# Softmax of a graph attention layer on 80 partitions instead of 8, merged with the edge sums, match matrices built one stage earlier

## The reference

```python
h = (x @ W.T).reshape(n, h_, d_)
e = leaky_relu(e_src + e_dst, 0.2) * (1.0 + et_emb[edge_type]) * edge_weight[:, None]
e_max = zeros((n, h_)).at[dst].max(e)          # largest logit of each destination and head, at least 0
e = exp(e - e_max[dst])
e_sum = zeros((n, h_)).at[dst].add(e)
alpha = e / (e_sum[dst] + 1e-10)
msg = h_src * alpha[:, :, None]
out = zeros((n, h_, d_)).at[dst].add(msg)      # then + x, a layer norm, gamma, beta
```

## Time and profile before

| | us |
|---|---|
| median of three runs (lowest, highest) | 2835.7 (2834.29, 2839.29) |
| the profiled execution's own time | 2833.69 |
| its span in the trace | 2832.0 |
| message stage, first instruction to the barrier's end | 1617.2 to 1842.5 |
| softmax stage | 1842.5 to 1891.7 |
| sums stage | 1891.7 to 1967.9 |

### The profile page before, as it was taken

One profiled execution on the slowest core, in us unless ns is written; L12 is line 12 of the kernel. 1 busy time (PEld: TensorE's weight loads), 2 busy tenths in 40 slices (PEclk: granted clock), 3 DMA queues, 4 the chain that ended last, 5 costly groups with the idle time before them and its releaser, 6 DMA issues. The chain is left out here.

```text
span 2832.0 us, 39727 instructions
## 1 busy us (share of the span) xinstructions
PE 2395.1 (85%) x13447; PEld 2050.2 (72%) x13447; DVE 1575.8 (56%) x3039; ACT 1093.6 (39%) x1874; POOL 856.0 (30%) x734
## 2 busy tenths in 40 slices
PE   5979999999999599999999799935777267999466
PEld 5969898989989599999999688824332155777355
DVE  4643233232323466666666533377799666777554
ACT  2233333333434233343333356623565353333232
POOL 1001010101000211111111134328898345665566
PEclk9989999999999799999999889968888688999788
DMA  6101010101002422333333234305466385776444
GB/s 218 37 8 56 19 56 19 51 19 44 26 23 49 159 104 104 112 110 104 118 138 119 86 102 118 89 25 198 140 224 226 130 260 187 260 263 233 154 152 130
DMA packets 118708, 330.52 MB, mean 117 GB/s; under 512 B 25981, under 2 KB 39293, under 8 KB 100571
## 3 DMA queue, kind: packets, MB, share of 16 engines
q1 hardware_dynamic: 69128, 228.79, 22.3%
q0 software_dynamic: 42976, 99.29, 12.2%
q10 hardware_dynamic: 6530, 1.53, 0.3%
HBM read 247.97 MB, written 128.49 MB: 133 GB/s over the span
## 5 line engine op out<-in xcount | busy, mean ns | idle before, releaser
L136 PE MATMUL b_y_ps<-W23h,b_Rh 128*128 128x320 f32 x800 | 249.5, 312 | 0.0
L138 PE MATMUL b_y_ps<-W23h,b_Rl 128*128 128x320 f32 x800 | 246.1, 308 | 0.0
L137 PE MATMUL b_y_ps<-W23l,b_Rh 128*128 128x320 f32 x800 | 246.0, 308 | 0.0
L537 POOL DMA_INDIRECT b_X<-in_x,b_idx x40 | 40.1, 1002 | 630.4 <-PE b_tp_ps L717 619.8
L911 POOL DMA_INDIRECT c_G<-T,c_idx x80 | 83.8, 1047 | 455.2 <-DVE c_U L1012 432.9
L136 PE MATMUL b_hid_ps<-b_hTh,W1h 128*128 128x512 f32 x500 | 200.6, 401 | 7.9 <-ACT b_Rh L586 7.9
L136 PE MATMUL c_u_ps<-c_W3h,c_hTh 128*128 128x320 f32 x640 | 200.8, 314 | 0.0
L137 PE MATMUL b_hid_ps<-b_hTl,W1h 128*128 128x512 f32 x500 | 199.3, 399 | 0.0
L138 PE MATMUL b_hid_ps<-b_hTh,W1l 128*128 128x512 f32 x500 | 199.2, 398 | 0.0
L138 PE MATMUL c_u_ps<-c_W3h,c_hTl 128*128 128x320 f32 x640 | 197.7, 309 | 0.0
L137 PE MATMUL c_u_ps<-c_W3l,c_hTh 128*128 128x320 f32 x640 | 197.7, 309 | 0.0
(11 more groups left out here) (378 smaller groups left out, 6971.7 us busy)
## 6 DMA issues: line engine op xcount, KB each, us to landing
c_X<-in_x SPq DMA_DIRECT2D x21, 1024.0 KB, 5.2
x<-n_O SPq DMA_DIRECT2D x20, 1032.0 KB, 4.9
g_X<-x SPq DMA_DIRECT2D x20, 1032.0 KB
x<-c_XB SPq DMA_DIRECT2D x20, 1028.0 KB, 3.9
n_X<-x SPq DMA_DIRECT2D x20, 1028.0 KB, 7.4
x<-g_O SPq DMA_DIRECT2D x20, 1024.0 KB, 3.9
c_XB<-in_x SPq DMA_DIRECT2D x19, 1024.0 KB
out<-g_B SPq DMA_DIRECT2D x19, 1024.0 KB, 4.8
```

Source lines behind the costliest of these rows:

```text
L136: pe.matmul(out, ah, bh, start=first, stop=False)
L137: pe.matmul(out, ah, bl, start=False, stop=False)
L138: return pe.matmul(out, al, bh, start=False, stop=last)
L537: pool.indirect_dma_start(X[:, i // GROUP, i % GROUP, :], None, a["x"][:, :], bass.IndirectOffsetOnAxis(idx[:, i:i + 1], 0), bounds_check= ...
```

## The change

1. Softmax and sums become one stage, `layer1_sums`, without the barrier between them. `logit` now has the shape 128 x (4 tiles of a group, 8 heads, 10 groups), so that the 80 columns of one j are turned at once: four transposes give `L` as 80 partitions (head by group, a "chunk") with 512 edge places each.
2. `same`, the two scans, the subtraction and Exp run on 80 x 512. A scan starts anew in each chunk, so the maxima have to be carried over: two scans of `same` alone (`left`, `right`) say whether a place is linked to the chunk's edge; four small matmuls bring the four edge values of each chunk to one partition (`rows`, 1 x 320); two scans over 80 values there chain the chunks (`before`, `after`); two matmuls bring the results back to 80 partitions (`cols`); and two passes apply `top = max(link * col, top)`.
3. ScalarE runs Exp once on a single column at the stage's start (`warm`), ahead of the copy of the logits.
4. The probabilities are split into `Ph` and `Pl` once for all tiles. GpSimd's copy of 8 columns goes; `Y`, `Yh` and `Yl` are 512 wide; the matmuls with `match` and `heads` become 256 wide, and each tile gets four more matmuls with 8 columns. The product reads its 8 factors at a distance of 10 elements.
5. The ten instructions that build `match` move to the start of the message stage.

```diff
@@ layer1_messages, vector @@
-                    dve.tensor_tensor(logit[:, bass.ds(g * 4, GROUP), :], dots[:, :, :], keep["fac"][:, bass.ds(g * 4, GROUP), :],
-                                      ALU.mult).then_inc(dot_read, 1)
-
+                    dve.tensor_tensor(logit[:, :, :, bass.ds(g, 1)], dots[:, :, :].unsqueeze(3),
+                                      keep["fac"][:, bass.ds(g * 4, GROUP), :].unsqueeze(3), ALU.mult).then_inc(dot_read, 1)
+
+                for g in range(EG):
+                    w = slice(g * GROUP, (g + 1) * GROUP)
+                    dve.tensor_tensor(match[:, w, :], keep["rows"][:, g * (GROUP * P):(g + 1) * (GROUP * P)].rearrange("p (j q) -> p j q", q=P),
+                                      over(keep["dst"][:, w].unsqueeze(2), [P, GROUP, P]), ALU.is_equal).then_inc(built, 1)
                 split_on_dve(dve, Wraw[:, :, :], Wh[:, :, 0:F], Wl[:, :, 0:F], w_hi, 1, w_lo)
...
@@ layer1_sums (layer1_softmax is gone); CH = EG * HEADS = 80, CW = GROUP * P = 512 @@
+        L, top = sb("L", [CH, CW]), sb("top", [CH, CW])
+        same = sb("same", [CH, CW + 1], U16)
+        left, right = sb("left", [CH, CW]), sb("right", [CH, CW])
...
             def _(act):
+                act.activation(warm[:, :], keep["eps"][:, 0:1], ACT.Exp)
+                act.wait_ge(turned, 1)
+                act.copy(L[:, :], turn[0:CH, :]).then_inc(flat, 1)
+                act.wait_ge(shifted, 1)
+                act.activation(L[:, :], L[:, :], ACT.Exp).then_inc(exped, 1)
+                act.wait_ge(prob_ready, 2)
+                act.copy(Ph[:, :, :, :], logit[:, :, :, :]).then_inc(p_hi, 1)
...
             def _(pool):
-                pool.wait_ge(init, 1)
+                pool.wait_ge(prob_ready, 2)
...
-                                           over(prob[:, bass.ds(t, 1), :].rearrange("p o h -> p (o h)").unsqueeze(2), [P, HEADS, HD]),
+                                           over(logit[:, j, :, bass.ds(g, 1)], [P, HEADS, HD]),
                                            ALU.mult).then_inc(weighed, 1)
-                        pool.tensor_copy(Y[:, j, :, F:F + HEADS], prob[:, bass.ds(t, 1), :]).then_inc(weighed, 1)
...
             def _(dve):
...
+                dve.tensor_tensor_scan(left[:, :], on, on, 1.0, ALU.mult, ALU.mult).then_inc(linked, 1)
+                dve.tensor_tensor_scan(right[:, ::-1], on_back, on_back, 1.0, ALU.mult, ALU.mult).then_inc(linked, 1)
+                dve.wait_ge(flat, 1)
+                dve.tensor_tensor_scan(top[:, :], on, L[:, :], 0.0, ALU.mult, ALU.max).then_inc(local, 1)
+                dve.wait_ge(local, 1)
+                dve.tensor_tensor_scan(top[:, ::-1], on_back, top[:, ::-1], 0.0, ALU.mult, ALU.max).then_inc(local, 1)
+
+                dve.wait_ge(rows_ready, 1)
+                dve.tensor_copy(rows[:, :], turn[0:1, 0:4 * CH]).then_inc(rows_out, 1)
+                dve.wait_ge(rows_out, 1)
+                tails, through, firsts, through_back = (rows[:, k * CH:(k + 1) * CH] for k in range(4))
+                dve.tensor_tensor_scan(before[:, 1:CH + 1], through, tails, 0.0, ALU.mult, ALU.max).then_inc(chained, 1)
...
+                dve.wait_ge(cols_ready, 1)
+                dve.tensor_copy(cols[:, :], back[0:CH, 320:324]).then_inc(cols_out, 1)
...
+                dve.scalar_tensor_tensor(out=top[:, :], in0=left[:, :], scalar=cols[:, 0:1], in1=top[:, :],
+                                         op0=ALU.mult, op1=ALU.max).then_inc(topped, 1)
...
+                dve.tensor_tensor(L[:, :], L[:, :], top[:, :], ALU.subtract).then_inc(shifted, 1)
+                dve.wait_ge(back_ready, 1)
+                dve.tensor_copy(flat_prob, back[:, 0:GROUP * CH]).then_inc(prob_ready, 1)
+                dve.wait_ge(prob_ready, 1)
+                dve.memset(flat_prob[0:1, :], 0.0).then_inc(prob_ready, 1)
+                dve.wait_ge(p_hi, 1)
+                dve.tensor_tensor(Pl[:, :, :, :], logit[:, :, :, :], Ph[:, :, :, :].bitcast(F32), ALU.subtract).then_inc(p_lo, 1)
...
             def _(pe):
+                for j in range(GROUP):
+                    mm = pe.transpose(turn[0:CH, j * P:(j + 1) * P], flat_prob[:, j * CH:(j + 1) * CH], keep["ident"][:, :])
+                mm.then_inc(turned, 1)
+                pe.wait_ge(local, 2)
+                pe.wait_ge(linked, 2)
+                for k, col in enumerate((top[:, CW - 1:CW], left[:, CW - 1:CW], top[:, 0:1], right[:, 0:1])):
+                    mm = pe.matmul(turn[0:1, k * CH:(k + 1) * CH], col, keep["ident"][0:CH, 0:CH], start=True, stop=True)
+                mm.then_inc(rows_ready, 1)
...
+                        share = s[:, 2 * (j % RS) + 1, GW:GW + HEADS]
+                        pe.matmul(share, own, Ph[:, j, :, g], start=True, stop=False)
+                        pe.matmul(share, own, Pl[:, j, :, g], start=False, stop=True).then_inc(sum_ready, 1)
```

More of the change, by code:

```diff
@@ L1158, in _, with layer1_messages @@
                         turn_rows(r + 1, (2 * j, 2 * j + 1))
[L1162 removed]
+def layer1_messages(nc, core, a, keep, x1, msg, logit, match):
     sem = core.sem
     w_loaded, w_hi, w_lo, diag_set = sem("d_w"), sem("d_whi"), sem("d_wlo"), sem("d_diag")
[L1166 removed]
+    proj_ready, built = sem("d_proj"), sem("d_built")
     idx_staged, go = sem("d_idx"), sem("d_go")
@@ L1402, in head_matrix, with layer1_sums @@
                              over(keep["dst"][:, 0:ET].unsqueeze(2), [P, ET, ET]), ALU.is_equal)
-def layer1_softmax(nc, core, a, keep, logit, match):
+def layer1_sums(nc, core, a, keep, msg, logit, match, T1):
     sem = core.sem
[L1408 to L1466, removed]
@@ L1470, in layer1_sums @@
-def layer1_sums(nc, core, a, keep, msg, prob, match, T1):
-    sem = core.sem
+    ids_loaded, same_ready, linked = sem("s_ids"), sem("s_same"), sem("s_linked")
+    turned, flat, local, rows_ready, rows_out, chained = (sem("s_" + n) for n in ("turned", "flat", "local", "rows", "rowsout", "chain"))
+    cols_ready, cols_out, topped, shifted, exped, back_ready = (sem("s_" + n) for n in ("cols", "colsout", "top", "shift", "exp", "back"))
+    prob_ready, p_hi, p_lo = sem("s_prob"), sem("s_phi"), sem("s_plo")
@@ L1485, in layer1_sums @@
         T = sb("T", [P, GROUP, F])
+        turn = core.ps(st, "e_turn_ps", [P, 512])
+        back = core.ps(st, "e_back_ps", [P, 512])
         s = core.ps(st, "e_s_ps", [P, 2 * RS, 512])
@@ L1488, in layer1_sums @@
         half = HEADS // 2
+        flat_prob = logit[:, :, :, :].rearrange("p j h g -> p (j h g)")
         with nc.Block() as block:
@@ L1521, in _ @@
                                            ALU.mult).then_inc(weighed, 1)
-                        pool.tensor_copy(Y[:, j, :, F:F + HEADS], prob[:, bass.ds(t, 1), :]).then_inc(weighed, 1)
             @block.vector
             def _(dve):
-                dve.memset(prob[0:1, :, :], 0.0).then_inc(init, 1)
+                dve.memset(before[:, 0:1], 0.0).then_inc(init, 1)
+                dve.memset(after[:, CH:CH + 1], 0.0).then_inc(init, 1)
                 dve.memset(zeros[:, :], 0.0).then_inc(init, 1)
@@ L1568, in _ @@
             def _(pe):
+                for j in range(GROUP):
[6 more added lines that the diff above has]
+                mm.then_inc(rows_ready, 1)
+                pe.wait_ge(init, 2)
+                pe.wait_ge(chained, 2)
+                for k, row in enumerate((before[:, 0:CH], after[:, 1:CH + 1])):
+                    mm = pe.matmul(back[0:CH, 320 + 2 * k:322 + 2 * k], row, keep["ident"][0:1, 0:2], start=True, stop=True)
+                mm.then_inc(cols_ready, 1)
+                pe.wait_ge(exped, 1)
+                for j in range(GROUP):
+                    mm = pe.transpose(back[:, j * CH:(j + 1) * CH], L[:, j * P:(j + 1) * P], keep["ident"][0:CH, 0:CH])
+                mm.then_inc(back_ready, 1)
                 pe.sem_inc(y_lo, GROUP)
@@ L2568, in program @@
                     msg = core.sb(w, "msg", [P, ET, F + HEADS])
-                    logit = core.sb(w, "logit", [P, ET, HEADS])
-                    core.run(layer1_messages, a, keep, x1, msg, logit)
-                    core.run(layer1_softmax, a, keep, logit, match)
+                    logit = core.sb(w, "logit", [P, GROUP, HEADS, EG])
+                    core.run(layer1_messages, a, keep, x1, msg, logit, match)
                     core.run(layer1_sums, a, keep, msg, logit, match, T1)
```

52 lines of the change are left out of this document (39 added, 13 removed).

## The result

The changed kernel takes 2811.4 us (median of four runs, 2804.0 to 2813.1), the kernel before 2837.5 beside it: a ratio of 0.9908, 95% interval 0.9894 to 0.9921. That is 26.1 us faster, where 35.0 were forecast (a median of 2800.5), and outside the stated range of 2796 to 2807.5. The profiled execution took 2803.98 us (span 2802.3), the fastest of the four.

A forecast was written before the change was run, and what follows sets the result against it. The softmax stage was taken as one chain, mostly VectorE's, with time going by elements along a partition. 36.8 us gained up to the first scaling less 1.8 in the loop gives 35.0: median 2800.5 us, range 2796 to 2807.5.

The forecast's parts named there:

- the mis-sized term: Sums loop: GpSimd's product starts late after VectorE's split and reaches into the next, 36 tiles, 0.4 us in all.
- The products that get in first: Early sums loop: two or three products go ahead of a split, until GpSimd is four tiles ahead; 1.7 us.
- Up to the first product: Stage start to first product's end: 15.9 us instead of 52.4, so 36.5 us earlier.
- the four one-column steps on TensorE: Carrying the maxima over: four one-column matmuls bring edge values to one partition, 0.7 to 1.1 us, taken as 0.85.
- First product to first scaling: Before the loop: first scaling 4.9 us after the first product's end, 5.26 before; stage mark 20.8 us instead of 57.6.
- The match matrices: Message stage: the moved 6.1 us cost nothing; the rival that they delay it gave 2806.8 us, chance 0.05.
- The dear carrying-over: Rival, softmax chain: carrying maxima over costs much more, gain only 28 us with the loop at +5, 2807.5; chance 0.08.
- TensorE as the bound: Rival, sums loop: twelve matmuls a tile set a beat of 1.9 us, 10 us lost, 2810.7; chance 0.05.
- Factors 10 elements apart: Rival, sums loop: GpSimd reads spaced factors slowly; a product of 2.2 us loses 48 us, 2848; chance 0.02.
- Each tile, the product goes ahead of each split: Rival, sums loop: every split delayed 0.85 us, 34 us over 40 tiles, 2834.7, no change; chance 0.01.
- hardly at all: Forecast's case for the loop: late products reach into the next split by 0 to 0.1 us; gain 33 to 37.5, chance 0.76.
- fully: Rival's case for the loop: a product holds off every split, 0.85 us each, 2834.7 us; chance 0.01.

The follow-up runs named there:

- e2: Changed kernel, each GpSimd product also waiting for the scaling of six tiles before: 2807.2 us, ratio to the kernel before 0.9893.
- e7: Changed kernel, each GpSimd product also waiting for the scaling of five tiles before: 2804.2 us, ratio to the kernel before 0.9882.
- e1: Changed kernel with an idle GpSimd copy of 8 columns behind each product again: 2805.5 us, ratio to the kernel before 0.9878.
- e3: Kernel before with GpSimd's copy of 8 columns taken out of the loop (divisors wrong): 2845.6 us, ratio to the kernel before 1.0037.
- e8: Changed kernel, split multiplying Y by a cleared PSUM tile instead of subtracting Yh (low part zero): 2796.7 us, ratio to the kernel before 0.9862.
- e5: Changed kernel with the ten match instructions back in the sums stage, behind e_heads: 2819.1 us, ratio to the kernel before 0.9934.
- e4: Changed kernel with only one of each tile's four added 8-column matmuls (divisors incomplete): 2808.7 us, ratio to the kernel before 0.9901.
- e6: Changed kernel run again without any edit: 2813.0 us, ratio to the kernel before 0.9912.

## Why the prediction was wrong

It was right on direction, on the order of the chain and on the kind of loss in the loop, and wrong on two sizes. By the trace, 35.0 us less the two misses below, 7.6 in the loop and 2.8 ahead of the first scaling, gives 24.6; the stretch has 24.6, the medians 26.1.

- *The loop: the mis-sized term.* I wrote that GpSimd, once four tiles ahead, starts a product "about 0.05 us later than the split let go" and reaches into the next split "by 0 to 0.1 us", 0.4 us in all; with the rest +1.8 us for the loop, bound +5. Measured: the product starts 0.28 us after the split's end, the split grows by 0.24 in 32 tiles, and this term is 7.7 us, not 0.4; the loop grows by 9.4 (63.0 to 72.4). Redone with 0.28 in place of 0.05, and my own 0.9 us for which a product holds a split off, the sum comes out: 0.28 + 0.9 less the 0.95 us from one split's end to the next split's start is 0.23. The products that get in first, priced at 1.7 us, are as forecast in the changed kernel: two beats, 0.84 us each. The added wait leaves one of them at six tiles (e2) and none at five (e7).
- *Why I missed it.* I had seen what decides it: in the earlier trace rows the next product starts right behind a copy that the split holds up. I took the hand-over by a semaphore for 0.05 us, which is what most hand-overs among VectorE, ScalarE and TensorE show in the earlier trace rows. For GpSimd the trace of before had other numbers. The first product of the sums (1892.47) starts 0.48 us after the memset of `logit` (ended 1891.99), whose semaphore it waits for by the code; the row names the instruction behind it, `e_zeros`. And in the third layer's node stage GpSimd waits 20 times for VectorE (`g_B` at line 2043 for `g_O` at line 2135); five of these that I read, the first from 2377.94 to 2378.20, took 0.20 to 0.27 us. e1, e2 and e7 remove the loss by the moment of release alone, e3 makes it in the kernel before, e8 removes it by the second input. What the 0.28 us consist of stays open: between its wait and the product GpSimd also raises a semaphore (`go`), and no run leaves that out.
- *Up to the first product: 17.4 us instead of 14.75.* The load of `e_ids` lands late and holds up `same` for 1.25 us (I said nothing of that load); the four one-column steps on TensorE and their hand-over take 1.26 instead of 0.85, the two column ones 0.70 instead of 0.55; the small scans 0.2 more, the large ones 0.2; and GpSimd wakes 0.46 us after the memset, again not 0.05. The rest matched: three passes 2.3 against 2.2, Exp 0.68 against 0.7, the four transposes back 0.83 against 0.95. ScalarE loads no table between the subtraction and Exp.
- *First product to first scaling: 6.15 us*, forecast 6.05. VectorE does get in between two products when it waits: its first three splits take 4.06 us together, about as laid out.
- *The match matrices*: free, as forecast (e5).
- *Rivals.* The dear carrying-over: dearer by 0.8 us (its matmuls and small scans, above), not by 3.5. TensorE as the bound: refuted (e4; e1). Factors 10 elements apart: the product takes 1.06 instead of 1.04 us, and e3, with factors side by side, has the same beat. "Each tile, the product goes ahead of each split" had the right place, a collision in nearly every tile, at 0.85 us each; that is so in two tiles, and in 32 it is 0.24, since a product that starts late only reaches into the split. That middle case had no chance of its own: I gave chances only to "hardly at all" and "fully".

## What to carry to other kernels

Where two engines share a port, the gap between their instructions is part of the loop's design. Taking work off the engine that isn't the bound can cost time, if that work was what kept it standing in the queue at the right moment. Before removing such an instruction, ask what will release the next one and when, and whether it still ends before the bound engine needs the port. One more wait, on an event that falls inside the other engine's instruction, can set it right (stretch 316.3 us against 326.1).

A chain of short steps is priced by its hand-overs. Read them for each pair of engines, in another stage of the same trace if the stage at hand has none, and include the load that the first step needs.

## What the runs showed of the hardware

- GpSimd starts 0.27 to 0.29 us after the end of the VectorE instruction that it waits for in the loop (0.46 after the memset; 0.20 to 0.27 in another stage of the kernel before). VectorE, ScalarE and TensorE mostly follow each other in 0.03 to 0.06 us; TensorE behind a scaling took 0.15 (1904.08 to 1904.23) and behind the second small scan 0.14.
- With a copy held up by a split, the product queued behind it starts 0.02 us after the split's end (e1). A product issued while a split runs is through 0.91 us after the split's end (e2), where one alone takes 1.06.
- A VectorE instruction with both inputs in SBUF and a GpSimd product delay each other (split 0.93 us, product 1.24); with one input in PSUM they don't, at the same size (0.68 and 1.06, e8).
- Gathers issued by GpSimd beside VectorE's two-input match instructions took 1.20, 1.47 and 1.50 us (again in e6) instead of 1.01 to 1.04 (e5).
- A scan takes 10.81 us for 8x5120 and 1.19 to 1.22 us for 80x512: its time goes by the elements along a partition, not by the number of partitions.
